# Further products of constants on TensorE, in a graph-and-experts kernel

## What is computed

```python
x = x + gnn(_layernorm(x), W, src, dst, edge_weight)
    # h = x @ W.T;  msgs = edge_val[:, None] * h[edge_col];  segment_sum(msgs, edge_row)
x = x + ffn(_layernorm(x))
    # two of 16 experts by a gate, relu(x @ w1 + b1) @ w2 + b2, weighted, added, layernorm
```

## Time and profile before

| | us |
|---|---|
| timed runs | 2364.69, 2383.14, 2874.64 |
| median | 2383.14 |
| profiled execution | 2405.79 |
| its span | 2404.0 |
| busy PE, DVE, ACT, POOL | 1508.3, 970.1, 645.8, 1204.3 |

### The profile page before, as it was taken

How to read it: one execution, slowest core, us unless ns; L and a number is a source line. 1 busy time by engine, 2 the same in 40 slices (tenths; PEclk the granted TensorE clock), 3 DMA queues, 4 the chain that set the end, 5 groups by cost and what they waited for, 6 DMA issues and landing times. The chain is left out here.

```text
span 2404.0 us, 33977 instructions
## 1 busy us (share of the span) xinstructions
PE 1508.3 (63%) x7875; PEld 1206.6 (50%) x7876; DVE 970.1 (40%) x2547; ACT 645.8 (27%) x1788; POOL 1204.3 (50%) x1170
## 2 busy tenths in 40 slices
PE   5256977564445565555565546464644799998975
PEld 3245866452334343333343434343433799897864
DVE  7995799472112222222222132121317333332338
ACT  5741266330000110101010100101015344443456
POOL 0045558786655555555555444545552355454434
PEclk9595589686668676877677767677876999999988
DMA  4112212224522222222222222222236222224346
GB/s 154 62 54 82 77 52 66 72 66 142 179 79 72 70 70 70 70 70 70 70 70 70 70 61 65 72 66 74 72 70 190 86 71 77 94 85 159 118 145 229
DMA packets 121466, 215.63 MB, mean 90 GB/s; under 512 B 21001, under 2 KB 82756, under 8 KB 121281
## 3 DMA queue, kind: packets, MB, share of 16 engines
q0 software_dynamic: 52864, 140.45, 19.9%
q1 hardware_dynamic: 53664, 56.14, 7.0%
q10 hardware_dynamic: 14880, 18.35, 2.3%
HBM read 172.32 MB, written 42.54 MB: 89 GB/s over the span
## 5 line engine op out<-in xcount | busy, mean ns | idle before, releaser
L470 POOL DMA_INDIRECT hbuf<-xn_rows,ix x640 | 614.9, 961 | 574.2 <-DVE ix L420 217.8
L549 PE MATMUL bank<-hbuf,picks 128*128 x1640 | 535.1, 477 | 549.8 <-SPq L458 274.4
L549 PEld LDWEIGHTS bank<-hbuf,picks 128*128 128x128 f32 x1640 | 363.6, 237 | 714.1 <-issue 660.4
L491 DVE TENSOR_SCALAR picks<-iota_two,marks 128x256 f32<-128x256 f32 x640 | 239.5, 420 | 920.6 <-remote 616.4
L737 POOL DMA_INDIRECT fbuf<-xn_rows,first_tables x196 | 230.1, 1174 | 130.0 <-PE bank L1261 66.9
L627 ACT ACTIVATE agg<-bank 128x256 f32<-128x256 f32 x49 | 18.8, 385 | 863.3 <-PE bank L549 565.5
L1845 PE MATMUL bank<-rowsT,w_sb 128*128 128x128 f32 x1744 | 216.3, 278 | 19.1 <-issue 19.1
L1845 PEld LDWEIGHTS bank<-rowsT,w_sb 128*128 128x128 f32 x1744 | 212.2, 193 | 31.0 <-issue 26.3
L1855 PE MATMUL bank<-w_sb,hT 128*128 128x256 f32 x872 | 209.2, 382 | 0.9 <-ACT hT L1803 0.6
L1781 POOL DMA_INDIRECT expert_out<-y_sb,to_i x112 | 111.4, 995 | 192.6 <-DVE y_sb L1890 188.0
L1279 PE MATMUL bank<-work 128*128 128x192 bf16 x1568 | 154.8, 254 | 75.2 <-DVE work L1067 57.1
(11 more groups left out here) (293 smaller groups left out, 1729.0 us busy)
## 6 DMA issues: line engine op xcount, KB each, us to landing
w_sb<-in_L_ffn_w_dram ACTq DMA_DIRECT2D x28, 512.0 KB
hbuf<-xn_rows,ix POOLq DMA_INDIRECT x640
first_sums<-x SPq DMA_DIRECT2D x49, 128.0 KB
first_sums_back<-first_sums SPq DMA_DIRECT2D x7, 896.0 KB
xn_rows<-xn SPq DMA_DIRECT2D x7, 896.0 KB, 4.6
x<-in_x_dram SPq DMA_DIRECT2D x6, 896.0 KB
ya<-expert_out SPq DMA_DIRECT2D x5, 896.0 KB, 5.3
yb<-expert_out SPq DMA_DIRECT2D x5, 896.0 KB, 7.2
```

Of the source, the lines that this page charges most:

```text
L470: pool.indirect_dma_start(hbuf[:, 1 + j, k, :], None, xn_dram, bass.IndirectOffsetOnAxis(ap=ix[:, 2 * j + k:2 * j + k + 1], axis=0)).then_ ...
L491: s = v.tensor_scalar(picks[:, j % 2, k, :], iota_two[:], marks[:, 0, 2 * j + k:2 * j + k + 1], marks[:, 1, 2 * j + k:2 * j + k + 1], ALU. ...
L549: m = nc.tensor.matmul(bk[q][:, 0:D], picks[:, j, k, q * P:(q + 1) * P], hbuf[:, ds(place + j, 1), k, :].rearrange("p s d -> p (s d)"), st ...
```

## The change

PE makes products of two constants whose results nobody reads: `ident` times `iota_two`, 256 columns in 32-bit floats, two at a time. They are made in three places: in the loop of the second gather, behind each pair's wait for `pair_in` and ahead of its own products; in `sum_to` for the 60 static tiles behind the batches, ahead of each tile's waits; and once per block of nodes in the placing, behind `gate_x`. The transposes of the sorted records use five banks by turns instead of six, since `bk[7]` is now written by the products.

```diff
-        TURNED = 6
+        TURNED = 5
@@ gather_tensor
-            def quad(s, q):
+            def quad(s, q, kept_busy):
                 place = s & (PR - 1)
                 for j in range(2):
                     pe.wait_ge(pair_in, s + j)
+                    if kept_busy:
+                        for k in range(2):
+                            nc.tensor.matmul(bk[6][:, 0:2 * P], ident[:], iota_two[:], start=True, stop=True)
                     for k in range(2):
@@ window
-                    for m in quad(s, q):
+                    for m in quad(s, q, True):
                         m.then_inc(used, 1)
-                for m in quad(end, q):
+                for m in quad(end, q, False):
@@ sum_to
-                def sum_to(tiles):
+                def sum_to(tiles, kept_busy=False):
...
+                        if kept_busy:
+                            for k in range(2):
+                                nc.tensor.matmul(bk[7][:, 0:2 * P], ident[:], iota_two[:], start=True, stop=True)
                         pe.wait_ge(first_picked, used + 1)
@@ the tensor block
                         gate_x(w - 1)
+                        for k in range(2):
+                            nc.tensor.matmul(bk[5][:, 0:2 * P], ident[:], iota_two[:], start=True, stop=True)
...
-                sum_to(SORT_TILES + 16)
+                sum_to(SORT_TILES + 16, True)
...
-                sum_to(FTILES)
+                sum_to(FTILES, True)
```

## The result

The changed kernel takes 2530.14 us, the median of 4 runs (2528.47 to 2543.71), against 2385.49 us for the kernel before, the median of 4 runs (2364.69 to 2874.64). The ratio, which leaves out the run of 2874.64 as disturbed, is 1.065, 95% interval 1.0568 to 1.0732: **slower**. The profiled execution took 2530.24 us, its span 2528.5 us, 124.5 us longer than the span of the profile before. The medians are 144.65 us apart: the profile before stands 20 us above its median (2405.79 against 2385.49), the one after does not.

The account below looks back on a forecast made before the run. Waits bound the kernel, no engine being near full: PE's instructions complete late while POOL issues gathers. 2405.79 + 176 + 25 - 8 = 2599 us profiled, less 22.65 to the median, 2576 us; range 2290 to 2690.

Parts of the forecast that it names:

- rival 1: Whole kernel: the forecast as made, with more or less of 4.4 us per half turn; 2470 to 2690 us, chance 0.55.
- Second gather, +176 us: Second gather: constants add 4.4 us to each of 40 half turns, +176 us; bounds -374 and +524.
- The pair left over: Second gather: one pair fewer completes during POOL's run, adding 2.6 us, about half covered; 1.4 us per half turn.
- The longer catching up: Second gather, behind POOL's run: pairs with constants take 1.0 us more each, 3.0 us for three.
- The lateness counts instructions: PE while POOL issues gathers: late completion goes by instructions, not columns, 0.7 to 0.85 us each.
- Rival 2: Second gather: lateness grows with every new instruction, 9 us per half turn staying, 360 us; about 2760 us, chance 0.07.
- Static tiles, +25: 60 static tiles behind the batches: four more matrix instructions each cost +25 us; bounds -10 and +115.
- five banks, 0: Transposes of sorted records: five banks instead of six cost 0, at most +4 us.
- Placing, -8: Placing, 48 blocks: a warm clock makes a block 1.97 us instead of 2.13, -8 us; cold it would be +80.
- (3), hidden: Whole kernel: the constants use slack that PE has; 2383 us, within 2%, chance 0.14.
- (4), the clock pays: Second gather: a raised clock shortens work without constants, -98 us, +20 for tiles, lateness staying; 2305 us, chance 0.11.
- (5), the lateness goes: Second gather: dense, warm PE loses its lateness and keeps up with POOL, -374 us, +20; 2029 us, chance 0.13.

Follow-up runs that it names:

- g2: Against the kernel before: constant products in the second gather alone, 16 columns instead of 256; 2531.25 us against 2404.03, ratio 1.0513.
- f2: Against the kernel before: constant products in the 60 static tiles behind the batches alone, with five banks; 1991.58 us, ratio 1.0152.
- b: The kernel before, unchanged, run again for its profile on a chip with prompt completions; 1960.81 us, one run.
- e1: Against the kernel before: constant products of 256 columns in the second gather alone, six banks; 1993.45 us, ratio 1.014.
- f1: Against the kernel before: constant products in the placing alone, two per block of nodes; 1979.18 us, ratio 1.0096.
- a: The changed kernel, unchanged, run again beside the kernel before on a chip with prompt completions; 2010.48 us against 1962.5, ratio 1.0185.
- e2: Against the kernel before: constant products in the placing and static tiles alone, with five banks; 1998.97 us, ratio 1.0207.
- e3: Against the kernel before: constant products in the second gather alone, 16 columns instead of 256; 1967.26 us, ratio 1.0037.
- e4: Against the kernel before: constant products in the second gather alone, placed ahead of each pair's wait instead of behind it; 1969.61 us, ratio 1.0067.
- g1: Against the kernel before: constant products of 256 columns in the second gather alone, repeated on another chip; 1968.58 us, ratio 1.0056.
- occasions 1 to 3: The first three follow-up sessions, each on another chip, completions prompt; the kernel before took 1953 to 1987 us.
- occasion 2: The second follow-up session, where both kernels were run again unchanged; 2010.48 us for the changed kernel against 1962.5 for the kernel before.

## Why the prediction was right, and where it wasn't

The prediction, 2576 us with a range of 2290 to 2690, was 46 us above the 2530.14 measured, and its forecast (rival 1) is what happened. Some of the closeness is luck: in terms of profiles it said 2599 us, 69 above the 2530.24 measured, and forecast +193 where the profiles show +124.5 and the medians +145. It took off 22.65 us because the profile before stands above its median; the one after has no such distance, so this hid a third of the error. By its steps:

**Second gather, +176 us: mechanism right, size too large, +125 measured.** POOL's gap grows by 3.24 us per half turn, not 4.4. The prediction's two terms both are there. The pair left over was put at 1.4 us; behind POOL's run stand 0.6 pairs more (3.63 to 4.24), at 1.82 us a pair before 1.1 us. The longer catching up was put at 3.0 us; a pair takes 2.24 us instead of 1.82 (the third row of the table by the fourth), for 4.24 pairs 1.8 us. That is the term that was mis-sized: I had taken half of the constants cold and half warm for three pairs; in the half turn shown only the first pair is cold. DVE's going on comes 0.4 us later (3.20 to 3.62). The second gather is 1316 us long, less than the 1330 to 1380 that were to show it.

**The lateness counts instructions: borne out, not isolated.** It rested on two intervals of rows 5. The 16 columns of g2 give the same gap to a tenth of a us, which excludes a price by the column; but that evenness has the clock in it too. Rival 2, in which every instruction pays fully (0.7 us for each, 9 us a half turn left), is nearly three times too large: 3.24 us were left.

**Static tiles, +25, and five banks, 0: the tiles near, the transposes wrong.** The tiles cost 4.8 + 14.5 = 19.3 us in the result, and 19.5 in f2 on another occasion. But the last tile ends only 7.5 us later, 3.3 of it handed on from the batches, because the transposes between the tiles took 15.1 us less. Their lateness had been put at nothing. Three rows of before, then two of the changed kernel:

```profile
552.98 2.82 PE L1310 MATMUL bank<-ident,work 128*128 128x128 f32 x12 [1.89 <-issue]
566.51 0.29 DVE L1080 COPY tables<-bank 128x128 f32<-128x128 f32 x1 [15.76 <-remote]
567.86 0.66 PE L1310 MATMUL bank<-ident,work 128*128 128x128 f32 x2 [12.06 <-issue]
561.07 1.25 PE L1318 MATMUL bank<-ident,work 128*128 128x128 f32 x10
561.49 0.29 DVE L1083 COPY tables<-bank 128x128 f32<-128x128 f32 x1 [2.46 <-issue]
```

Before, DVE sees the first table 13.5 us behind the start of the transposes, a late completion; in the changed kernel 0.4 us behind it. Before, POOL issues gathers without a break from 515 to 566 us; in the changed kernel it breaks off twice ahead of the transposes (idle 2.55 us before 552.04 and 1.89 before 554.88, this one for a tile of PE's). That the breaks let PE catch up fits the prediction's picture, but no run tests it. g2, with six banks and no constants there, has the long form too (19.3 us), so the banks and the constants are not told apart. With prompt completions the transposes take 5.0 us in f2 against 3.6 in b, within the 4 us allowed.

**Placing, -8: a warm clock right, the gain smaller and its sign a matter of what the placing was before.** The changed kernel, ten us of the placing:

```profile
230.00:240.00 10.00, 10.00 (x62) 8.97 (x61) 6.82 (x16) 2.35 (x7) 5.19 (x6) 1.00 0.31 97
```

62 products of 11.8 to a block are 1.90 us per block; I had said 1.97. Before, 39 products in ten us, 7.9 to a block, are 2.03 us, not the 2.13 of the prediction, so a warm block gains 0.13 us and 48 of them 6. The stage gave 3.3 us, not 8, and more than that was lost again in the batches, which the change doesn't touch: the last one ends 3.3 us later. What the prediction missed is that this stage of the kernel before has more than one form. In the profile that it was read from, and in that of e1, PE is full at 0.50 for most of it. In b the same code runs at 0.86 and takes 76 us, and there the constants cost 19 us (f1, a). With late completions PE has a hole as well: from 200 to 220 us it is busy 8.0 of 20 us before and 9.7 in the changed kernel, against 17.8 in b. The placing of e1 and of g2, whose code is that of the kernel before:

```profile
186.00:288.00 102.00, 101.33 (x379) 87.37 (x380) 77.60 (x178) 23.59 (x65) 65.95 (x62) 0.50 0.32 93
186.00:288.30 102.30, 82.73 (x379) 69.03 (x378) 75.99 (x179) 22.79 (x65) 67.05 (x62) 0.67 0.32 93
```

The 26 us between 262.0 and 288.1 match the two heights of the kernel before, 1958 and 1983. Its runs at the lower height have a mean granted clock of 0.874 to 0.883 over the whole kernel, those at the upper one 0.856 to 0.866, and the 18 runs of the kernels whose placing has constants (e2, a, f1) show one height each. So the heights are most likely the two placings, and the constants leave only the warm one; no run of the kernel before at 1983 was profiled to show it outright.

**The rivals.** (3), hidden: wrong where completions are late; with prompt ones the second gather is close to it, +7 to +9 us of 812 (e1, e3, e4, g1, a), and the whole kernels e3 and g1 are 0.4 and 0.6% longer. (4), the clock pays: the clock rose to 0.82 from 0.74, and beside g2, at 0.73, that was worth about the columns of the constants and no more. The prediction cited the Trainium skill, TensorE: Matmul & The Clock Gate, What's actually happening, that activity releases the throttle; here it was released in part only: PE still stands idle for 12.46 us in the half turn shown, and is at 1.2 GHz behind it. (5), the lateness goes: not by the change, but for the transposes above. On occasions 1 to 3 it was gone without the change, and then the second gather is POOL-bound as this rival had it (its 806 us, 812.3 measured in b). So its picture was right and its cause wrong: b has it without any of the constants, and the changed kernel of the result lacks it with all of them.

**What was to show it.** POOL's idle time grew as said (574.2 to 713.1), but not under the name forecast: the part put down to `ix` fell from 217.8 to 38.6 us, and that put down to PE rose to 469.4. The name of a releaser is the last event by the profile; the sum of the group is what could be forecast. DVE's waits for something remote in the changed kernel are 575.2 us. POOL's, in total, times, longest:

```profile
POOL hbuf L470 <- PE bank L552: 469.4, 47, 24.5
POOL hbuf L470 <- DVE ix L420: 38.6, 4, 10.0
```

DVE stands 18.62 us until POOL's run is over, as said. The constants take 0.26 us each warm and 0.52 cold (1.03 and 2.07 for four), where 0.2 to 0.4 was said.

## What to carry to other kernels

Work that keeps TensorE busy is free only where TensorE is waited for by nobody: ask at each place whether it runs into a wait or stands behind one, and what bounds the stage next. Where completions were late, narrowing such products saved nothing (g2); whether fewer of them would, no run tells. Before forecasting from one profile, look whether a stage of it could have run in another mode: here both the placing's clock and PE's completions did, and the kernels with late ones take some 425 us longer (2385 against 1960), three times what the change costs.

## What was not expected of the hardware

**The same kernel took 1953 to 1987 us on three occasions and 2364 to 2420 us on two (beside one run of 2874.64).** The difference lies in the second gather mostly (1176 us from first to last gather in the profile before, 812 in b, of 445 between their spans; 62 lie ahead of it), and comes with PE's effects being seen up to 15 us after their modelled ends while POOL issues gathers at one per 1.26 us. POOL's gathers themselves take the same (961 and 966 ns). What decides it is not shown: no experiment turned it on or off, and in the result and on occasion 2 both kernels have it or lack it together. Each further occasion had another chip, so chip and time aren't told apart either. The Trainium skill, NOTIFIC — the notification-queue block, section Overflow: three behaviours, one of which stalls the engine, names a way in which records of a profile hold an engine back. No run here speaks for or against it.

**TensorE stayed at 1.2 GHz while it was busy 101.33 of 102 us** (e1's placing, above), and ran at 0.86 on average in another run of the same code with PE busy 63.07 of 76. With two more products per block it was 0.91 in the changed kernel and 0.97 in a and f1. So the busy share of the profile alone doesn't tell the granted clock.
